# Two attention layers and a mixture of experts: context and residual rows split into halves before a DMA transpose, and the stages spread over more steps

## What is computed

```python
x = x + xattn(layernorm(x), ctx_1024, ...)   # q from x; k, v from the context; 16 heads of 16, rope, causal softmax, Wo
x = x + gla(layernorm(x), ...)               # gated linear attention: q, k (16x8), v (16x16), decay, head norm, silu gate, Wo
x = x + ffn(layernorm(x), ...)               # one shared expert and the 2 best of 7 routed experts, hidden size 704
```

## Time and profile before

| | |
|---|---|
| time of the profiled run | 1832.72 us |
| its span | 1830.9 us |
| its mean granted TensorE clock | 0.965 |
| median of the three timed runs | 1831.21 us |
| TensorE matmul busy | 1613.1 us (88%) |
| TensorE weight load busy | 1209.7 us (66%) |
| VectorE busy | 1379.9 us (75%) |
| ScalarE busy | 911.7 us (50%) |
| GpSimd busy | 655.7 us (36%) |

### The profile page before, as it was taken

One profiled execution on the slowest core, in us unless ns is written; L12 is line 12 of the kernel. 1 busy time (PEld: TensorE's weight loads), 2 busy tenths in 40 slices (PEclk: granted clock), 3 DMA queues, 4 the chain that ended last, 5 costly groups with the idle time before them and its releaser, 6 DMA issues.

```text
span 1830.9 us, 45927 instructions
## 1 busy us (share of the span) xinstructions
PE 1613.1 (88%) x17692; PEld 1209.7 (66%) x17692; DVE 1379.9 (75%) x2756; ACT 911.7 (50%) x2456; POOL 655.7 (36%) x785
## 2 busy tenths in 40 slices
PE   6789889889898888898898885849999999999987
PEld 3566666656665656666666663648788888888866
DVE  3899999989999999999999974837544444444456
ACT  2566666676665666666666652215322222222221
POOL 3353433434433434334334320570133333333220
PEclk8999999999999999999999986879999999999999
DMA  4021010010010010100100000426322222222271
GB/s 118 18 68 38 20 39 21 20 39 21 28 32 20 21 38 21 39 21 21 39 20 21 25 5 20 111 61 173 87 71 70 73 71 72 71 70 71 59 244 64
DMA packets 118208, 97.96 MB, mean 54 GB/s; under 512 B 67728, under 2 KB 106272, under 8 KB 118000
## 3 DMA queue, kind: packets, MB, share of 16 engines
q1 hardware_dynamic: 107248, 61.86, 12.8%
q0 software_dynamic: 10752, 33.17, 5.3%
HBM read 62.49 MB, written 18.35 MB: 44 GB/s over the span
## 4 chain that ended last, share of the span: by engine, by line
PE 45%; DVE 42%; issue 6%; POOL 4%; ACT 2%; DMA 2%; SPq 0%; DVEq 0%; POOLq 0%
PE ps L945 19%; PE ps L972 9%; PE ps L637 6%; PE ps L645 5%; DVE experts L1329 4%; PE ps L632 3%; POOL experts L581 3%; DVE experts L1564 3%; DVE experts L1340 2%; DVE work L1411 2%; DVE work L1614 1%; DVE experts L1554 1%; DVE work L1496 1%; DVE experts L1634 1%; DVE work L1513 1%
## 5 line engine op out<-in xcount | busy, mean ns | idle before, releaser
L945 PE MATMUL ps<-work,experts 128*128 128x256 f16 x3564 | 408.5, 276 | 28.3 <-DMA work<-token_in 13.3
L945 PEld LDWEIGHTS ps<-work,experts 128*128 (+1 forms) x3564 | 344.9, 99 | 82.9 <-issue 11.6
L632 PE MATMUL ps<-cst,experts 128*128 128x128 f32 x1696 | 244.6, 281 | 50.5 <-DVE experts L1599 29.9
L637 PE MATMUL ps<-experts 128*128 128x512 f32 (+1 forms) x640 | 282.8, 565 | 3.5 <-DMA experts<-in_L_xattn_bv 3.4
L1035 ACT ACTIVATE work<-work 128x768 f16<-128x768 f32 x108 | 91.0, 843 | 370.7 <-PE ps L977 235.9
L1035 ACT ACTIVATE experts<-ps 128x512 f16<-128x512 f32 (+2 forms) x416 | 227.3, 582 | 89.7 <-PE ps L632 88.1
L548 POOL TENSOR_TENSOR experts<-experts,cst 128x128 f32<-128x128 f32 x256 | 152.7, 633 | 307.3 <-DVE experts L1554 307.3
L632 PEld LDWEIGHTS ps<-cst,experts 128*128 128x128 f32 x1696 | 195.9, 144 | 99.9 <-issue 51.0
L1043 ACT ACTIVATE experts<-ps,experts 128x256 f32<-128x256 f32 x512 | 235.1, 479 | 43.8 <-DVE experts L1329 43.8
L972 PE MATMUL ps<-experts,work 128*128 (+1 forms) x1620 | 198.6, 276 | 3.7 <-DVE work L1749 3.7
L972 PEld LDWEIGHTS ps<-experts,work 128*128 128x128 f16 x1620 | 155.3, 99 | 30.0 <-DVE work L1749 4.4
(11 more groups left out here) (191 smaller groups left out, 2768.6 us busy)
## 6 DMA issues: line engine op xcount, KB each, us to landing
experts<-in_ctx SPq DMA_DIRECT2D x32, 512.0 KB, 4.0
experts<-choice_out POOLq DMA_DIRECT2D x8, 1024.0 KB, 14.4
experts<-in_x SPq DMA_DIRECT2D x32, 128.0 KB, 3.6
token_in<-experts SPq DMA_DIRECT2D x32, 128.0 KB, 3.1
work<-in_L_ffn_routed_gate SPq DMA_DIRECT2D x8, 352.0 KB, 3.0
work<-in_L_ffn_routed_up SPq DMA_DIRECT2D x8, 320.0 KB, 4.2
out<-x_all POOLq DMA_DIRECT2D x5, 512.0 KB, 3.4
experts<-in_L_ffn_routed_gate SPq DMA_DIRECT2D x6, 352.0 KB, 3.0
```

The source lines that it names most:

```text
L632: ins = pe.transpose(bank[:, k * P:(k + 1) * P], a, ident)
L637: ins = pe.matmul(bank, lhs[k], rhs[k], start=(k == 0), stop=(k == len(lhs) - 1))
L945: ins = pe.matmul(out, experts_h[:, e, lo:lo + P], e_rows_t[k][:, b * DK + kk, :], start=(kk == 0 and a + b == 0), stop=(kk == DK - 1 and ...
```

## The change

- **Context.** ScalarE takes the float16 high half of the rows as loaded (`context_high`, 1024 elements for each of 128 partitions), GpSimd the low half (`context_low`), and one DMA transpose from SyncE turns both (`turn_context`, 16 blocks of 128x128). The 8 transposes on TensorE and the two ScalarE copies are gone.
- **Keys and values.** `w_kv` is split into scaled float16 halves once; a tile is one bias product (64 rows, 512 columns) and six float16 matmuls of 512 columns in place of two float32 ones. `kv_bias_0` to `_3` become scaling copies on ScalarE.
- **Residual rows.** `x1_norm` stays; high half on ScalarE from SBUF, low half on GpSimd, transpose by DMA (`turn_x1n`). `x1` and `g_v` have two buffers.
- **Gate.** The bias is a product too (one more matmul in `project_vg`); `gate_out` is gone, ScalarE takes the exponential and `gate_silu` the product straight from PSUM; `g_values_out` moves to ScalarE.
- **Moved from VectorE to GpSimd:** `g_query_heads`, `x1n_low`, `k_add`, `x2_norm`, `x_norm`.
- **Order.** All step lists are new, lags go to 7 on TensorE and to 14 on ScalarE, STEPS is 46. The PSUM banks of many functions change.
- **Routing.** `lane_hot` is written by VectorE, in two instructions of 32x128 elements, in tiles 1 and 2 (`lanes_of`).

```diff
@@ SyncE
+        def turn_context(p):
+            sp.wait_ge(S["ctx_high_ready"], p + 1)
+            sp.wait_ge(S["ctx_low_ready"], p + 1)
+            wait(sp, S["kv_done"], 4 * p)
+            apart(sp)
+            sp.dma_start_transpose(ctx_t.rearrange("p a m n -> p (a m) n"), ctx_s.rearrange("p a t n -> p (a t n)"))\
+                .then_inc(S["ctx_turned"], 16)
+        def turn_x1n(p):
+            sp.wait_ge(S["x1n_hi_ready"], p + 1)
+            sp.wait_ge(S["x1n_lo_ready"], p + 1)
+            apart(sp)
+            sp.dma_start_transpose(x1n_t.rearrange("p a k n -> p (a k) n"), x1n_s.rearrange("p a n -> p (a n)"))\
+                .then_inc(S["x1n_turned"], 16)
         def step(s):
-            at(s, 7, store_x2n)
+            if s >= 5:
+                at(s, 3, load_x)
+            at(s, 2, turn_context)
+            at(s, 10, store_x2n)
             if s >= 2:
                 at(s, 1, load_context)
-            if s >= 3:
-                at(s, 1, load_x)
+            at(s, 5, turn_x1n)
@@ GpSimd
         def step(s):
-            at(s, 1, residual)
-            at(s, 0, masks_of)
-            at(s, 3, split_x2n)
-            at(s, 0, rope_k)
-            at(s, 0, rope_q)
-            at(s, 0, v_low)
+            at(s, 8, g_query_heads)
+            at(s, 5, rope_k)
+            at(s, 7, x1n_low)
+            at(s, 6, residual)
+            at(s, 5, k_add)
+            at(s, 5, rope_q)
+            at(s, 5, v_low)
+            at(s, 4, masks_of)
+            at(s, 3, context_low)
+            at(s, 10, split_x2n)
+            at(s, 9, x2_norm)
+            at(s, 4, x_norm)
...
-        pool.wait_ge(S["route_step"], ROUTE_PARTS)
-        for c in range(TOPK):
-            for t in range(NTILE):
-                ins = nc.gpsimd.tensor_scalar(lane_hot[:, c, t, :], const("iota"), r_lane[:, c, t:t + 1], None,
-                                              ALU.is_equal)
-            ins.then_inc(S["lane_hot_ready"], 1)
@@ TensorE
+        def bias_product(bank, at):
+            pe.matmul(bank, pick[0:SQ, :], bias_s[0:SQ, at:at + 2 * D], start=True, stop=False)
-        def project_kv_1(p):
-            pe.wait_ge(S["ctx_t_ready"], 2 * p + 2)
...
-            product(ps[:, 6, :], [ctx_t[:, k, 1 * P:2 * P] for k in range(DK)], [w_kv[:, k, :] for k in range(DK)],
-                    S["kv_done"])
+        def project_kv_1(p):
+            pe.wait_ge(S["ctx_turned"], 16 * p + 16)
+            wait(pe, S["exp_done0"], 4 * p - 2)
...
+            bias_product(ps[:, 1, :], 0)
+            split_product(ps[:, 1, :], [[ctx_t[:, a, 2 + k, :] for k in range(DK)] for a in range(2)], blocks(w_kv_s),
+                          S["kv_done"], False)
+            at(s, 0, project_kv_0)
+            at(s, 2, turn_heads_0)
+            at(s, 2, weigh_values_1)
+            at(s, 1, scores_0)
+            at(s, 4, turn_g)
...
+            at(s, 2, project_out)
+            at(s, 0, project_kv_1)
+            at(s, 1, turn_probs_0_1)
+            at(s, 0, turn_xn)
+            at(s, 3, project_vg)
+            at(s, 3, g_scores)
...
+            at(s, 2, project_qk)
+            at(s, 0, turn_k_0)
+            at(s, 0, turn_q)
+            at(s, 2, project_decay)
@@ ScalarE
+        def context_high(p):
+            act.wait_ge(S["ctx_loaded"], 16 * p + 16)
+            if p <= 2:
+                wait(act, S["ctx_turned"], 16 * p)
+            nc.scalar.activation(ctx_s[:, 0], ctx_rows, ACT.Copy).then_inc(S["ctx_high_ready"], 1)
+        def kv_bias_0(p):
+            act.wait_ge(S["kv_done"], 4 * p + 1)
+            wait(act, S["v_split"], p)
+            nc.scalar.activation(kv[:, 0, :], ps[:, 5, :], ACT.Copy, scale=1 / W_SCALE).then_inc(S["kv_ready"], 1)
@@ VectorE
+        def lanes_of(c):
+            v.tensor_tensor(lane_hot[:, c, :, :], bc(r_lane[:, c, :], 2, P), bc(const("iota"), 1, NTILE), ALU.is_equal)\
+                .then_inc(S["lane_hot_ready"], 1)
             if t <= TOPK:
+                lanes_of(t - 1)
                 half_of(t - 1)
-STEPS = NPAIR + 7
-SPLIT_STEP = 2
+STEPS = NPAIR + 14
+SPLIT_STEP = 7
```

More of the change, by code:

```diff
@@ L210, in program @@
     row_inv = [place(8) for _ in range(2)]
-    x1 = place(D)
+    x1 = [place(D) for _ in range(2)]
     x1n = place(D)
-    x1n_s = halves(DK, P)
-    g_v = place(D)
-    gate = place(D)
+    x1n_s = place(D).bitcast(F16).rearrange("p (a n) -> p a n", a=2)
+    g_v = [place(D) for _ in range(2)]
     gate_e = place(D)
@@ L639, in product, with split_product @@
                 ins.then_inc(done, 1)
-        def split_product(bank, lhs, rhs, done, last=True):
+        def split_product(bank, lhs, rhs, done, first=True):
             for k in range(len(lhs[0])):
                 for a, b in ((0, 0), (0, 1), (1, 0)):
-                    ins = pe.matmul(bank, lhs[a][k], rhs[b][k], start=(k == 0 and a + b == 0),
+                    ins = pe.matmul(bank, lhs[a][k], rhs[b][k], start=(first and k == 0 and a + b == 0),
                                     stop=(k == len(lhs[0]) - 1 and a == 1))
@@ new lines, in project_kv_3, with project_out @@
+        def project_kv_3(p):
+            pe.wait_ge(S["ctx_turned"], 16 * p + 16)
+            wait(pe, S["heads_t_ready1"], p - 1)
+            if p == 0:
+                pe.wait_ge(S["kv_split"], 5)
+            bias_product(ps[:, 6, :], 0)
+            split_product(ps[:, 6, :], [[ctx_t[:, a, 6 + k, :] for k in range(DK)] for a in range(2)], blocks(w_kv_s),
+                          S["kv_done"], False)
+        def project_out(p):
+            pe.wait_ge(S["exp_done0"], min(4 * p + 5, 4 * NPAIR - 3))
+            pe.wait_ge(S["heads_t_ready1"], p + 1)
+            if p == 0:
+                pe.wait_ge(S["weights_loaded"], 16 * WEIGHT_DMAS)
+            product(ps[:, 2, :][:, 0:D], [heads_t[:, a, :, :].rearrange("p b i -> p (b i)") for a in range(2)],
+                    [w_o[:, a, :] for a in range(2)], S["proj_done"])
@@ new lines, in weigh_g_values, with project_q @@
+        def weigh_g_values(p):
+            pe.wait_ge(S["a_ready"], 4 * p + 4)
+            pe.wait_ge(S["g_v_ready"], p + 1)
+            pe.wait_ge(S["probs_lo_ready02"], min(p + 3, NPAIR))
+            apart(pe)
+            g_weigh(g_v[p % 2], ps[:, 7, :], S["go_done"])
+        def project_q(p):
+            wait(pe, S["probs_lo_ready00"], p)
+            pe.wait_ge(S["xn_t_ready"], p + 1)
+            if p == 0:
+                pe.wait_ge(S["q_loaded"], 32)
+            product(ps[:, 5, :][:, 0:D], [xn_t[:, k, :] for k in range(DK)], [w_q[:, k, :] for k in range(DK)], S["q_done"])
@@ new lines, in turn_probs_1_0, with turn_x2n, turn_probs_1_3 @@
+        def turn_probs_1_0(p):
+            pe.wait_ge(S["exp_done1"], 4 * p + 3)
+            turn_probs(ps[:, 2, :], 1, 0, S["probs_turned1"])
+        def turn_x2n(p):
+            pe.wait_ge(S["x2n_ready"], p + 1)
+            if p >= NPAIR - 3:
+                wait(pe, S["logits_ready"], p)
+            turn(ps[:, 5, :], [x2n[p % 2][:, k * P:(k + 1) * P] for k in range(DK)], S["x2n_turned"])
+        def turn_probs_1_3(p):
+            pe.wait_ge(S["exp_done1"], 4 * p + 4)
+            turn_probs(ps[:, 3, :], 1, 3, S["probs_turned1"])
```

1219 lines of the change are left out of this document (583 added, 636 removed).

## The result

The changed kernel takes 1657.31 us (median of 4 runs, 1656.37 to 1659.57) against 1831.84 us before: the ratio is 0.905, interval 0.903 to 0.908. The forecast was 1718 us, so the gain was 174 us and not 114. The profiled execution has a span of 1655.0 us, against 1830.9.

| Term | forecast, us | measured, us | read from |
|---|---|---|---|
| 31 periods between add_x1 of pair 0 and of pair 31 | -118 | -184.9 | 1039.1 before, 854.2 after |
| Start, up to add_x1 of pair 0 | +13 | +18.8 | 66.5, 85.3 after |
| End, from the last add_x1 to the routing | +5 | +7.2 | 35.7 before, 42.9 after |
| Slot table, from the routing to tile 4 | -14 | -16.9 | 89.9 before, 72.9 after |
| Expert tiles | 0 | 0.0 | 599.7 us in both |

A forecast was written before the change was run, and what follows sets the result against it. VectorE was taken to set the 33.52 us period, TensorE second. The sum was 1832.7 - 118 (periods) + 13 (start) + 5 (end) - 14 (slot table) = 1718 us; range 1665 to 1785 us, the forecast's own 1694 to 1743.

The forecast's parts named there:

- Start: Up to add_x1 of pair 0: first transpose waits behind all weight loads, first product near 29 us; +13 us (8 to 22).
- End: Last pair runs alone through the chain with a DMA transpose, a GpSimd subtraction and slower g_query_heads and x2_norm: +5 us.
- Slot table: Hole of 24.1 us before the slot product closes, two VectorE instructions of 4.5 us added: net -14 us (-9 to -17).
- the port waits: VectorE in each pair: 15 instructions wait for GpSimd, 0.6 us per meeting, 6.6 us in all, bringing VectorE to 29.9 us.
- the reach of TensorE: Period: the fullest engine reaches 95% of it, so TensorE's 27.8 us gives 29.2; 29.7 us chosen.
- Bound before: Kernel before: VectorE sets the period, busy 31.74 of 33.26 us (95%), with TensorE second, 2 us behind.
- VectorE's own work, 23.3 us: VectorE in each pair: 31.74 less 6.98 us of removed work is 24.8, and 23.3 without today's waits for GpSimd.
- TensorE 27.8 us: TensorE in each pair: 29.7 - 1.3 (transposes) - 0.8 (key and value tiles) + 0.2 (gate bias product) = 27.8 us.
- the dense rival: Periods: TensorE's 27.8 us reached within 1%, VectorE hides its waits; period 28.1, 1668 us; chance 0.16.
- Context transpose 9 us: SyncE's DMA transpose of the context: 4 x 1.26 + 4 = 9 us, with 16 us of cover.
- The contention rival: Periods: 15 VectorE instructions wait 0.6 us each, or x1n comes 2 to 3 us late; 1758 to 1805 us; chance 0.20.
- the slower ones: VectorE's 15 instructions wait 0.87 us each, 1927 us, chance 0.04; or context transpose takes over 22 us, chance 0.02.

The follow-up runs named there:

- b2: Kernel before, the four key and value bias additions taken from VectorE, ScalarE copying the tiles without bias: 1813.0 us.
- a6: Changed kernel with k_add, the addition of the rotated keys, on VectorE instead of GpSimd: 1740.3 us.
- a11: Changed kernel with the bias products contracted over all 128 rows (64 of them zero) instead of 64: 1649.3 us.
- a1: Changed kernel without the four bias products of keys and values: 1646.8 us.
- b1: Kernel before with only its lane table compared by VectorE in two instructions, as in the changed kernel: 1815.1 us.
- a4: Changed kernel with GpSimd's low half of the context taken over 16 of its 256 columns alone: 1654.5 us.
- a14: Changed kernel with bias products over 128 rows and GpSimd's context_low moved behind g_query_heads of the next step: 1627.7 us.
- a17: Changed kernel with context_low moved behind g_query_heads, bias products left at 64 rows: 1655.1 us.
- a10: Changed kernel with the first context's transpose and the second context's load issued before the 16 loads of w_o: 1654.3 us.
- a2: Changed kernel with one more VectorE instruction in each pair, a sum over 640 columns that nobody reads: 1670.1 us.
- a3: Changed kernel with three more VectorE instructions in each pair, sums over 640 columns that nobody reads: 1721.4 us.
- a8: Changed kernel with six more VectorE instructions in each pair, sums over 640 columns that nobody reads: 1806.1 us.
- a12: Changed kernel without the key and value bias products and with GpSimd's context low half over 16 of 256 columns: 1619.7 us.

## Why the forecast was 61 us too high

Two steps failed, and both are needed for the miss: the port waits (3) and the reach of TensorE (5). The forecast's period was 29.7 us and 27.55 were measured. Of the 2.15 us between them 0.5 are what was put on top of TensorE's 29.2 for VectorE's port waits, 1.1 are the 95% applied to TensorE (29.2 against 28.1), and 0.55 are TensorE's list and its last per cent (28.1 against 27.55): about 15, 34 and 17 us in 31 periods. The period's line of the sum missed by 67 us; start, end and slot table, 5 us above theirs together, took some of it back.

1. **Bound before** (VectorE at 95%): right, but incomplete. b2 shows a second bound 0.6 us below it, of waits.
2. **VectorE's own work, 23.3 us**: right. The port waits, read as each instruction's mean over its shortest in the same trace, come to 2.9 us a pair; with them it makes 26.2, and 26.2 were measured.
3. **VectorE's port waits, "15 x 0.6 x 21.5 / 29.5 = 6.6"**: this step failed. Measured were 2.9 us. Of these 1.15 are the two running sums (1.71 against 2 x 0.28), 0.41 g_gated, and the others 0.33 or less each. The mean over random meetings is the wrong model here: the order repeats, so each instruction meets the same thing in nearly every pair, most of them little or nothing and a few much. The same term could have been larger as well, as a6 shows with 1.45 us in one instruction.
4. **TensorE 27.8 us**: within 0.4 us (27.4 measured), but in part by luck. The bias product cost 0.32 us and mostly 0.10 more ahead of it, in place of 0.22; this was inside the bounds given, and makes 0.9 us in five. In a11, where it costs the 0.22 that the forecast charged, the whole list is 26.8 us, 1.0 under the forecast. Two misses cancel, and no run splits the second.
5. **"Today the fullest engine reaches 95% of it"**: this step failed too, for TensorE. The 95% are VectorE's (24 ns an instruction on the mean, waits included); TensorE reaches 99.4%. 27.8 / 0.95 = 29.2 should have read 27.8 / 0.99 = 28.1, the figure of the dense rival. This alone would not have lowered the forecast, for VectorE's 29.5 us stood above it; nor would the port waits alone have brought it below TensorE's 29.2. With the VectorE term right, 26.2 / 0.95 = 27.6 us is the other ceiling. Measured, TensorE's stands at 27.55 us and VectorE's at 27.4 (a1).
6. **ScalarE 24.6 us, GpSimd 21.5 us**: 23.3 and 21.0 measured (share times period), and neither holds anybody for long. **Context transpose 9 us**: 4.7. **x1n's path, 1 us of stall or less**: none.
7. **Start, end, slot table**: +18.8, +7.2 and -16.9 against +13, +5 and -14; all three within 6 us, and b1 reproduces the last by itself.

The dense rival was what came, with 0.16 against 0.55 for the forecast, and its 1668 us was still 11 too high. The range began at 1665, 3 us under that rival's one figure, and left no room for it to be too high. The contention rival and the slower ones did not come. The Trainium skill (SBUF — State Buffer, "Who interferes with whom") has whichever of the two engines issues first keep the shared ports for its whole instruction. That holds in the mechanism, as g_square's end behind v_low's in a6 shows, and does not say how often the two meet.

Left open: how much of the period's 6.0 us the longer lags brought by themselves. b2, with less VectorE work and more ScalarE work in the old order, gained 0.6 us of them; no run had the old work in the new order.

## What to carry to other kernels

Give each engine its own ceiling: read it from a stage in which that engine is the full one, and don't carry one engine's share over to another. Where two engines stand within a per cent of each other, take from both or expect little: here 10.5 and 3 us apart were 38 together, and the same move gave 2 us in one version and 22 in the next. In a periodic kernel look for port meetings in the timeline of two neighbouring pairs, by name, and move the long GpSimd instruction to where VectorE reads PSUM.

## What the runs showed of the hardware

- In a6 VectorE's g_square (two SBUF inputs), started 0.24 us behind GpSimd's v_low (2.17 us), ended 0.3 us after it: 2.22 us, and 0.42 at its shortest.
- Two running sums of 128x64 on VectorE took 1.71 us beside GpSimd's context_low (2.00 us), and 0.28 us each without it (a4, a14, a17).
- A float16 product over 64 rows and 512 columns among 128-row ones holds TensorE 0.32 us, the same over 128 rows 0.22; the instructions ahead of it hold it 0.10 us longer as well (0.96 against 0.86).
- A DMA transpose of the context (two halves) is issued in 2.0 us and lands 4.7 us after the issue began (median; 4.3 to 6.9); with 2.18 MB of another queue in flight it lands after 13.5 (a10).
- VectorE's busy share in a stage that it bounds is 94.0 to 95.7% (before, a1, a2, a3, a6, a8, a11, a12), TensorE's 99.1 to 99.4% (after, a4, a14, a17).
